# A two-layer graph network: how layer 0 of the kernel adds the rows of its edges per target node

## The chip, the cores and the metric

The kernel runs on one core of one Trainium2 chip. A core has five engines with an instruction stream each: PE (TensorE, matrix products), DVE (VectorE), ACT (ScalarE), POOL (GpSimd) and SP (SyncE, here only for issuing DMAs). They share the on-chip memory SBUF and the accumulator memory PSUM, and meet through semaphores. The metric is the device time of one execution in microseconds (us).

## The reference

12,500 nodes with 128 numbers each, 200,000 edges sorted by their target `dst`. Each layer normalises the nodes, sends a row along every edge, adds the rows per target, and applies two products.

```
h = relu(layernorm(x))
# layer 0
agg = segment_sum(h[src], dst, num_segments=12500)
x = x + (agg @ W_rel.T + b_rel + h @ W_root.T)
h = relu(layernorm(x))
# layer 1
edge_weights = silu(edge_attr @ We1 + be1) @ We2 + be2       # 50 -> 128 -> 128
agg = segment_sum(h[src] * edge_weights, dst, num_segments=12500)
x = x + (silu(agg @ Wn1 + bn1) @ Wn2 + bn2)
```

All of it is in fp32. A node has 16 incoming edges in the mean.

## The kernel before

**Tiles and stages.** The edges are cut into 391 blocks of 512, a block into 4 tiles of 128 edges, one edge per partition. Both layers run 23 iterations (`ITERS`) of 17 blocks (`U`). An iteration is cut into six groups (`G`) of three blocks (`GB`), the last group having two; a group is 12 tiles, the last 8, and 68 tiles make an iteration. For each group the lowest target is known (`sum_base`, `base_row`), and all of its targets are looked for in a window of 128 nodes from there. Were a group's targets spread wider, the whole layer would be run again with the windows moved by 128 (`passes`, from the table `plan` that DVE works out in the set-up).

**Gather (POOL).** `gather` issues one indirect DMA per tile, 68 per iteration (L320): 128 rows of 512 bytes into `rows`, which holds one iteration and is not doubled. Before the DMAs of group g POOL waits until the segment sums of the same group, one iteration earlier, have been signalled on `s_seg`. The indices come through SP (`load_idx`, L219) in two halves per iteration.

**Segment sum (DVE, PE).** For each group DVE's `one_hot` (L711) compares the targets in `dst_rel` with 0 to 127 and writes a 128x1536 one-hot matrix (1024 wide in the last group) into one of the two halves of `onehot`. PE's `segment_sum` (L370) multiplies each of the 12 tiles of rows by its one-hot tile and accumulates all of them in PSUM, in `seg_a` or `seg_b` by turns, and then signals `s_seg`. DVE's `add_window` (L719 to L723) waits for that and adds the 128x128 result to the right columns of `agg`. The order on DVE is written out by hand: `add_window` of group g-1, `one_hot` of group g+1, then a step of the node update.

**Set-up and the first iteration.** In the first 160 us the table of h = relu(layernorm(x)) is made for all nodes (`stats_of`, `shift_of`, `copy_h`: the h loop, 5 iterations of 5 node groups, L625 to L646), while POOL already gathers iteration 0 of layer 0. Since h is not ready then, iteration 0 gathers x and normalises the gathered rows itself (`edge_stats`, `edge_shift`, and ACT's relu; the edge phase). Iterations 1 to 22 gather from `h_rows`. Between its groups each of them also updates one group of 512 nodes (`node_update0`: ACT turns out `aggT`, PE makes 8 products L381 and L382 in group 1, DVE works on them in groups 3 to 5, L755 to L765). Three more updates follow the last iteration, then layer 1 begins.

**Layer 1.** The edge network (L410, L578, L416, L817, L825) makes each edge's message in `rows`, and `one_hot`, `segment_sum` and `add_window` add them as in layer 0.

## Time and profile before

| | us |
|---|---|
| median of 3 timed runs | 4831.68 (4816.43 to 4837.42) |
| the profiled execution's own time | 4849.66 |
| its span, first to last instruction | 4847.9 |
| POOL busy | 2970.8 (61%) |
| PE busy | 2418.4 (50%) |
| DVE busy | 1276.0 (26%) |
| ACT busy | 479.4 (10%) |

The profile is one execution. Its page gives each engine's busy time, the chain of work that ended last, and the costliest groups of instructions; the trace behind it gives each instruction with its start, its length, and how long the engine stood idle before it and for what. "remote" as a releaser means that the profile found no instruction on this core whose end fits the moment at which the waited semaphore rose; "issue" means that it shows nothing that the engine waited for. Times within the profile are counted from the span's start. The layers can be told apart by the lines: layer 0 ends on DVE at L704 and L705 near 2341 us.

### The profile page before, as it was taken

Reading aid. Unit: us, or ns where it says so; the run is one execution under the profiler, and the core shown is the slowest. Engines: PE = TensorE matmul, PEld = TensorE weight load, DVE = VectorE, ACT = ScalarE, POOL = GpSimd, SP = SyncE. Lnnn points to the kernel's source line nnn. Section 1 sums busy time; section 2 is a strip of 40 time slices with the busy share of each in tenths; the row PEclk is TensorE's granted clock in tenths of the full one; section 3 lists DMA queues with packets and bytes.
Section 4 is the critical chain, followed back from the end, with each engine's and each line's share of the span. In section 5 each row is a group of like instructions: output and inputs, shape, how many; then the busy total and the mean of one; then the engine's idle time right before and its main releaser. Section 6 shows DMA issues by size and latency. Waiting matters only on the chain.

```text
span 4847.9 us, 35780 instructions
## 1 busy us (share of the span) xinstructions
PE 2418.4 (50%) x10938; PEld 1841.8 (38%) x10938; DVE 1276.0 (26%) x2181; ACT 479.4 (10%) x842; POOL 2970.8 (61%) x3135
## 2 busy tenths in 40 slices
PE   1332323232323232322447677777666777767667
PEld 0322322232222222222334445555454555544545
DVE  2511111111111111111323333333333333333334
ACT  3400000000000000000101111111111111111111
POOL 5366666666666666666465656666656666656662
PEclk9755556555656565655667767777767777767777
DMA  5222222222221222222222222222222222222222
GB/s 135 61 53 52 55 53 56 54 53 53 56 54 51 56 55 54 51 56 55 62 59 61 65 62 64 65 69 64 65 61 64 65 67 66 64 61 64 64 63 59
DMA packets 230579, 296.77 MB, mean 61 GB/s; under 512 B 68580, under 2 KB 160278, under 8 KB 230433
## 3 DMA queue, kind: packets, MB, share of 16 engines
q0 software_dynamic: 100096, 205.20, 16.8%
q10 hardware_dynamic: 61378, 60.59, 4.6%
q1 hardware_dynamic: 69086, 30.79, 2.4%
q8 instruction: 6, 0.10, 0.0%
q14 instruction: 13, 0.10, 0.0%
HBM read 269.87 MB, written 26.48 MB: 61 GB/s over the span
## 4 chain that ended last, share of the span: by engine, by line
another core or an unknown queue 44%; PE 26%; issue 17%; DVE 10%; DVEq 2%; ACT 1%; POOL 0%; DMA 0%; ACTq 0%; SPq 0%; POOLq 0%
PE seg_a L370 7%; PE seg_b L370 5%; PE ew_a L416 4%; PE ew_b L416 3%; DVE onehot L711 3%; PE hid_b L410 3%; PE hid_a L410 2%; DVE ew_a L817 2%; DVE rows L825 2%; DVE ew_b L817 1%; DVEq L719 1%; PE node L430 0%; DVE e_stats L625 0%; PE node L381 0%
## 5 line engine op out<-in xcount | busy, mean ns | idle before, releaser
L320 POOL DMA_INDIRECT rows<-h_rows,idx x3060 | 2905.5, 950 | 1783.2 <-issue 952.2
L370 PE MATMUL seg_a<-onehot,rows 128*128 128x128 f32 x3312 | 662.9, 358 | 1136.9 <-DVE onehot L711 445.2
L370 PEld LDWEIGHTS seg_a<-onehot,rows 128*128 128x128 f32 x3312 | 601.9, 268 | 1221.4 <-issue 934.2
L370 PE MATMUL seg_b<-onehot,rows 128*128 128x128 f32 x2944 | 572.5, 340 | 809.3 <-issue 576.9
L370 PEld LDWEIGHTS seg_b<-onehot,rows 128*128 128x128 f32 x2944 | 504.8, 249 | 855.7 <-issue 659.9
L711 DVE TENSOR_TENSOR onehot<-iota_ps,dst_rel 128x1536 f32<-128x1536 f32 (+1 forms) x278 | 461.3, 1659 | 1.0 <-DVE dst_rel L699 0.6
L817 DVE TENSOR_TENSOR ew_a<-ew_a,be_all 128x512 f32<-128x512 f32 x207 | 144.6, 699 | 1044.7 <-remote 703.2
L416 PE MATMUL ew_b<-we_sb,hidden 128*128 128x128 f32 x1472 | 289.3, 357 | 224.6 <-ACT hidden L578 177.1
L416 PEld LDWEIGHTS ew_b<-we_sb,hidden 128*128 128x128 f32 x1472 | 245.2, 252 | 406.5 <-ACT hidden L578 210.3
L416 PEld LDWEIGHTS ew_a<-we_sb,hidden 128*128 128x128 f32 x1664 | 268.6, 245 | 246.3 <-issue 169.0
L416 PE MATMUL ew_a<-we_sb,hidden 128*128 128x128 f32 x1664 | 310.8, 345 | 81.4 <-ACT hidden L578 55.2
L723 DVE TENSOR_TENSOR agg<-seg_a,agg 128x128 f32 x138 | 40.3, 292 | 963.2 <-remote 883.0
L723 DVE TENSOR_TENSOR agg<-seg_b,agg 128x128 f32 x138 | 40.1, 290 | 866.1 <-remote 787.0
L817 DVE TENSOR_TENSOR ew_b<-ew_b,be_all 128x512 f32<-128x512 f32 x184 | 128.2, 697 | 508.1 <-remote 199.7
L578 ACT ACTIVATE hidden<-hid_a,be_col 128x512 f32<-128x512 f32 x208 | 142.9, 687 | 1106.9 <-remote 522.7
L578 ACT ACTIVATE hidden<-hid_b,be_col 128x512 f32<-128x512 f32 x185 | 126.9, 686 | 961.1 <-remote 486.7
L410 PE MATMUL hid_a<-ef_a,we_sb 50*128 50x512 f32 x278 | 196.9, 795 | 20.5 <-DMA ef_a<-ef_blocks 20.5
L410 PE MATMUL hid_b<-node_work,we_sb 50*128 50x512 f32 x230 | 173.1, 841 | 0.0
L825 DVE TENSOR_TENSOR rows<-ew_a,rows 128x512 f32<-128x512 f32 x207 | 143.2, 692 | 22.7 <-DMA rows<-h_rows,idx 13.2
L825 DVE TENSOR_TENSOR rows<-ew_b,rows 128x512 f32<-128x512 f32 x184 | 127.0, 690 | 7.9
L511 ACT ACTIVATE n_std<-n_mv,eps 128x4 f32<-128x4 f32 x25 | 7.4, 297 | 1041.4 <-issue 673.7
L523 ACT ACTIVATE hT<-agg 128x512 f32 x23 | 14.5, 629 | 851.3 <-DMA y_rows<-ys 845.7
(122 smaller groups left out, 1148.4 us busy)
## 6 DMA issues: line engine op xcount, KB each, us to landing
rows<-h_rows,idx POOLq DMA_INDIRECT x3060
ef_a<-ef_blocks ACTq DMA_DIRECT2D x70, 300.0 KB
node_work<-ef_blocks ACTq DMA_DIRECT2D x47, 300.0 KB
xs<-x SPq DMA_DIRECT2D x40, 256.0 KB
ys<-y_rows SPq DMA_DIRECT2D x26, 256.0 KB
out<-xs ACTq DMA_DIRECT2D x26, 256.0 KB
y_rows<-ys ACTq DMA_DIRECT2D x25, 256.0 KB
h_rows<-node_work ACTq DMA_DIRECT2D x23, 256.0 KB
```

Source lines behind the costliest of these rows:

```text
L320: pool.indirect_dma_start(out=rows[:, u, t, :], out_offset=None, in_=table, in_offset=bass.IndirectOffsetOnAxis(ap=idx[:, j:j + 1], axis=0 ...
L370: mm = pe.matmul(seg[g % 2][:, 0:P], rows[:, u, t, :], onehot[:, g % 2, k * TB + t, :], start=(k == 0 and t == 0), stop=(last and t == TB ...
L410: pe.matmul(hid_ps[u % 2][:, :], we1_sb[:, :], ef[g % 2][:, k, :], start=True, stop=True).then_inc(s_hid, 1)
L416: mm = pe.matmul(ew_ps[u % 2][:, t * D:(t + 1) * D], hidden[:, u % 2, t * P:(t + 1) * P], we2_sb[:, :], start=True, stop=True)
L511: nc.scalar.activation(n_std[:, r, :], n_mv[:, r, :, 1], ACT.Sqrt, bias=eps[:, :]).then_inc(s_nstd, 1)
L523: nc.scalar.activation(hT[r], h_table[:, bass.ds(g * BLOCK, BLOCK)], ACT.Copy)
L578: nc.scalar.activation(hidden[:, u % 2, :], hid_ps[u % 2][:, :], ACT.Silu, bias=be1_col[:, :]).then_inc(s_silu, 1)
L711: return v.tensor_tensor(onehot[:, g % 2, 0:tiles, :], iota_ps[:, 0:P].unsqueeze(1).to_broadcast([P, tiles, P]), dst_rel[:, bass.ds(it * U ...
L719: base = dve.value_load(base_row[0:1, bass.ds(it * G + g, 1)], min_val=0, max_val=BASE_MAX)
L723: v.tensor_tensor(window, seg[g % 2][:, 0:P], window, ALU.add).then_inc(s_acc[layer], 1)
L817: v.tensor_tensor(ew, ew, be2_all[:, :].unsqueeze(1).to_broadcast([P, TB, D]), ALU.add).then_inc(s_add, 1)
L825: v.tensor_tensor(rows[:, u, :, :], ew, rows[:, u, :, :], ALU.mult).then_inc(s_msg, 1)
```

## The change

In layer 0 the one-hot product over all tiles is replaced. The host arranges the edges so that a partition holds 12 neighbouring edges of the sorted list in each group (8 in the last group). Neighbours mostly have the same target, so a partition's 12 edges make a few runs of equal targets. `R = 3` runs are handled in one pass over the layer. In a new function `run_sums` DVE builds three masks of 12 columns in PSUM, `run_mask` (which edge belongs to which run), and a one-hot row for the target of each run, `run_hot` (128x384). Then, for each of the three runs, it multiplies the group's rows by the mask into a PSUM tensor of three banks (`wide`, 128x1536) and reduces that over the 12 edges into a 128x128 tile `run_sum`. The reduction reads PSUM with a stride of 128 numbers. PE then needs 3 products of 128x128 per group instead of 12 (8 in the last group). If a partition has more than three runs, the layer is run again with the next three (`passes0 = passes1 * ceil(runs / 3)`); the largest number of runs is worked out in the set-up.

What goes with it:

- POOL's gather in layer 0 waits on `s_sum`, which DVE's reductions raise, instead of PE's `s_seg`.
- DVE's `add_window` of group g-1 stands behind `run_sums` of group g. DVE now waits for the gathered rows; PE waits only for `s_sum`.
- The set-up counts the runs and finds their targets (`run_targets`, three rounds over the 1564 edge columns) ahead of the h loop, as now stand the clearing of `agg[0]`, the plan and the load of `dst_sb`.
- After a pass over layer 0 `next_turn` with one more `run_targets` takes the place of `next_pass`.
- `hid_a`, `hid_b` and `ew_a` of layer 1 become parts of `wide`; `iota_ps` shares a bank (`consts_ps`) with the masks. The rest of layer 1 is as before, with the edges in the new order.

```diff
+R = 3
+RUN_STEPS = 2 * R
+        run_now = consts_ps[:, P:P + R]
+        run_mask = consts_ps[:, 2 * P:2 * P + R * GB * TB].rearrange("p (r e) -> p r e", r=R)
+        wide = ctx.enter_context(nc.psum_tensor("wide", [P, GB * BLOCK], F32))
+        picked = wide[:, :].rearrange("p (e f) -> p e f", f=D)
...
@@ gather (POOL)
-                    hold(pool, s_seg[layer], i * G + (g + 1))
+                    if layer == 0:
+                        hold(pool, s_sum, runs_summed(i, g) - RUN_STEPS * G)
+                    else:
+                        hold(pool, s_seg[1], i * G + (g + 1))
...
@@ PE
+            def run_sums(i, g):
+                pe.wait_ge(s_sum, runs_summed(i, g))
+                for r in range(R):
+                    mm = pe.matmul(seg[g % 2][:, 0:P], run_sum[g % 2][:, r, :], run_hot[g % 2][:, r, :],
+                                   start=(r == 0), stop=(r == R - 1))
+                mm.then_inc(s_seg[0], 1)
...
@@ DVE, set-up
+            def run_targets(n):
+                for r in range(R):
+                    out = run_dst[:, :, r].rearrange("p (i g) -> p i g", g=G)
+                    v.scalar_tensor_tensor(scratch, run_of, run_now[:, r:r + 1], dst_flat,
+                                           ALU.is_equal, ALU.mult).then_inc(s_pass, 1)
+                    dve.wait_ge(s_pass, n + (2 * r + 1))
+                    v.tensor_reduce(out[:, :, 0:G - 1], per_run[:, :, 0:full].rearrange(
+                        "p i (g e) -> p i g e", g=G - 1), AX.X, ALU.max)
+                    v.tensor_reduce(out[:, :, G - 1], per_run[:, :, full:U * TB], AX.X, ALU.max).then_inc(s_pass, 1)
...
@@ DVE, layer 0
+            def run_sums(i, it, g):
+                dve.wait_ge(s_sum, done)
+                v.tensor_tensor(run_mask[:, :, 0:tiles],
+                                dst_rel[:, bass.ds(it * U + first, tiles // TB), :].rearrange("p k t -> p (k t)")
+                                .unsqueeze(1).to_broadcast([P, R, tiles]),
+                                run_now.unsqueeze(2).to_broadcast([P, R, tiles]),
+                                ALU.is_equal).then_inc(s_mask, 1)
+                v.tensor_tensor(run_hot[g % 2], iota_ps.unsqueeze(1).to_broadcast([P, R, P]),
+                                run_dst[:, bass.ds(it * G + g, 1), :].rearrange("p g r -> p (g r)").unsqueeze(2)
+                                .to_broadcast([P, R, P]), ALU.is_equal)
+                dve.wait_ge(s_mask, i * G + (g + 1))
+                for r in range(R):
+                    if r > 0:
+                        dve.wait_ge(s_sum, done + 2 * r)
+                    v.tensor_tensor(picked[:, 0:tiles, :],
+                                    rows[:, first:first + tiles // TB, :, :].rearrange("p k t f -> p (k t) f"),
+                                    run_mask[:, r, 0:tiles].unsqueeze(2).to_broadcast([P, tiles, P]),
+                                    ALU.mult).then_inc(s_sum, 1)
+                    dve.wait_ge(s_sum, done + (2 * r + 1))
+                    v.tensor_reduce(run_sum[g % 2][:, r, :], picked[:, 0:tiles, :].rearrange("p e f -> p f e"),
+                                         AX.X, ALU.add).then_inc(s_sum, 1)
...
                     for g in range(G):
+                        dve.wait_ge(s_rows[0][g], landed(i, g))
+                        run_sums(i, it, g)
                         if g > 0:
                             add_window(0, i, it, g - 1)
                         else:
                             add_window(0, i - 1, it - 1, G - 1)
-                        one_hot(it + (g + 1) // G, (g + 1) % G).then_inc(s_onehot, 1)
...
@@ host
+            order.append((first + g) * BLOCK + np.arange(P * tiles).reshape(P, tiles).T.ravel())
-    src_cols = src_pad.reshape(-1, P).T
+    src_cols = src_pad[order].reshape(-1, P).T
```

**DVE, one group of a layer-0 iteration.** Before, the row of DVE reads as follows from the one-hot of group 1 on; `TENSOR_LOAD base_row` fetches the window's column.

```order
233 L719 ISA
234 L719 TENSOR_LOAD base_row
235 L719 ISA x2
236 L721 ISA
237 L722 REGISTER_ALU [waits s_acc_done0]
238 L723 ISA [waits s_seg_done0]
239 L723 TENSOR_TENSOR agg<-seg_a,agg 128x128
240 L711 ISA
241 L711 TENSOR_TENSOR onehot<-iota_ps,dst_rel 128x1536
```

Of the changed kernel, the same place in the program, DVE on group 1 of an iteration:

```order
341 L824 ISA [waits s_rows0_1]
342 L825 ISA [waits s_sum]
343 L825 TENSOR_TENSOR consts_ps<-dst_rel,consts_ps 128x36
344 L830 ISA
345 L830 TENSOR_TENSOR onehot<-consts_ps,run_dst 128x384
346 L833 REGISTER_ALU
347 L837 TENSOR_TENSOR wide<-rows,consts_ps 128x1536 [waits s_mask]
348 L841 REGISTER_ALU
349 L842 TENSOR_REDUCE onehot<-wide 128x128 [waits s_sum]
...
360 L850 ISA [waits s_seg_done0,s_acc_done0]
361 L850 TENSOR_TENSOR agg<-seg_a,agg 128x128
```

The pair L837 and L842 stands there three times. Where DVE had two instructions per group with data to work on, it has nine, and the sum into `agg` now follows all of the group's own work.

**PE, groups 0 and 1 of a layer-0 iteration.** Before (`x11` is eleven more of the row above):

```order
85 L370 MATMUL seg_a<-onehot,rows 128x128 [waits s_rows0_0]
86 L370 MATMUL seg_a<-onehot,rows 128x128 x11
87 L378 ISA
88 L381 MATMUL node<-w_root_sb,hT 128x128 [waits s_nT]
89 L382 MATMUL node<-w_rel_sb,node_work 128x128
...
97 L370 MATMUL seg_b<-onehot,rows 128x128 [waits s_rows0_1,s_onehot]
98 L370 MATMUL seg_b<-onehot,rows 128x128 x11
```

and of the changed kernel:

```order
48 L399 MATMUL seg_a<-onehot 128x128 [waits s_sum]
49 L399 MATMUL seg_a<-onehot 128x128 x2
50 L415 ISA
51 L418 MATMUL node<-w_root_sb,hT 128x128 [waits s_nT]
52 L419 MATMUL node<-w_rel_sb,node_work 128x128
...
60 L399 MATMUL seg_b<-onehot 128x128 [waits s_sum]
61 L399 MATMUL seg_b<-onehot 128x128 x2
```

Nine of twelve products per group are gone; the node update's products stay where they were, ahead of the products of group 1.

## Rows read from the trace of the kernel before

**Rows 1.** Page, part 4: the chain that ended last, by engine.

```profile
another core or an unknown queue 44%; PE 26%; issue 17%; DVE 10%; DVEq 2%; ACT 1%; POOL 0%; DMA 0%; ACTq 0%; SPq 0%; POOLq 0%
```

**Rows 2.** Busy time by stretch (layer 0, layer 1): length, engines, clock, DMA share, GB/s.

```profile
500.00:2290.00 1790.00, 533.34 (x2752) 476.74 (x2752) 263.11 (x453) 57.31 (x130) 1181.26 (x1249) 0.58 0.21 54
2400.00:4800.00 2400.00, 1653.45 (x7061) 1177.52 (x7061) 795.23 (x1069) 300.85 (x425) 1463.45 (x1548) 0.71 0.25 64
```

**Rows 3.** Timeline of POOL, one layer-0 iteration: start, length, instruction, [idle before].

```profile
1026.44 0.95 POOL L320 DMA_INDIRECT rows<-h_rows,idx  x1 [6.83 <-remote]
...
1065.22 0.94 POOL L320 DMA_INDIRECT rows<-h_rows,idx  x1 [0.30 <-issue]
1072.55 0.94 POOL L320 DMA_INDIRECT rows<-h_rows,idx  x1 [6.39 <-remote]
...
1124.18 0.95 POOL L320 DMA_INDIRECT rows<-h_rows,idx  x1 [6.93 <-remote]
```

**Rows 4.** Timeline of DVE, the same iteration.

```profile
1071.92 0.29 DVE L723 TENSOR_TENSOR agg<-seg_b,agg 128x128 f32 x1 [34.80 <-remote]
...
1077.40 0.69 DVE L759 TENSOR_TENSOR xs<-node,xs 128x512 f32<-128x512 f32 x1
...
1123.54 0.29 DVE L723 TENSOR_TENSOR agg<-seg_a,agg 128x128 f32 x1 [39.14 <-remote]
```

**Rows 5.** Timeline of PE, the same iteration.

```profile
1047.82 0.37 PE L370 MATMUL seg_b<-onehot,rows 128*128 128x128 f32 x1 [1.73 <-issue]
...
1056.23 0.37 PE L370 MATMUL seg_a<-onehot,rows 128*128 128x128 f32 x1 [2.43 <-issue]
1059.04 0.37 PE L370 MATMUL seg_a<-onehot,rows 128*128 128x128 f32 x1 [2.44 <-issue]
...
1078.06 2.84 PE L370 MATMUL seg_a<-onehot,rows 128*128 128x128 f32 x24
```

**Rows 6.** Timeline of DVE in the set-up.

```profile
9.20 2.28 DVE L622 TENSOR_REDUCE hi_sb<-agg 128x4 int32<-128x2048 int32 x1
...
15.85 0.15 DVE L634 RECIPROCAL e_rstd<-e_std 128x4 f32<-128x4 f32 x1
20.47 0.16 DVE L636 SCALAR_TENSOR_TENSOR e_shift<-e_mv,e_rstd 128x4 f32<-128x4 f32 x1 [4.47 <-remote]
...
34.94 0.86 DVE L625 BATCH_NORM_STATS2 e_stats<-node_work 128x6 f32<-128x128 f32 x4
41.64 0.38 DVE L629 BATCH_NORM_AGGREGATE e_mv<-e_stats 128x2 f32<-128x6 f32 x4 [5.84 <-remote]
```

**Rows 7.** Timeline of DVE 19 us into an unbroken stretch of gathers in layer 0.

```profile
292.44 0.88 DVE L736 BATCH_NORM_STATS2 n_stats<-xs 128x6 f32<-128x128 f32 x4
293.42 0.38 DVE L740 BATCH_NORM_AGGREGATE n_mv<-n_stats 128x2 f32<-128x6 f32 x4
```

**Rows 8.** Timeline of POOL: iterations 0, 1 and 2 begin, and layer 0's last gather.

```profile
3.61 1.10 POOL L320 DMA_INDIRECT rows<-x,idx  x1 [2.17 <-issue]
...
174.34 0.95 POOL L320 DMA_INDIRECT rows<-h_rows,idx  x1 [85.83 <-PE seg_a L370]
...
273.27 0.94 POOL L320 DMA_INDIRECT rows<-h_rows,idx  x1 [6.41 <-remote]
...
2320.03 0.94 POOL L320 DMA_INDIRECT rows<-h_rows,idx  x1 [0.30 <-issue]
```

**Rows 9.** Timeline of DVE: memory cleared, targets, first and last one-hot of the edge phase.

```profile
143.87 10.72 DVE L656 MEMSET agg<- 128x12800 f32 x1 [2.62 <-issue]
...
159.11 1.60 DVE L695 TENSOR_TENSOR dst_rel<-dst_sb,sum_base 128x1380 f32<-128x1380 int32 x1 [1.63 <-issue]
...
161.60 1.76 DVE L711 TENSOR_TENSOR onehot<-iota_ps,dst_rel 128x1536 f32<-128x1536 f32 x1 [0.63 <-DVE dst_rel L699]
...
232.80 1.75 DVE L711 TENSOR_TENSOR onehot<-iota_ps,dst_rel 128x1536 f32<-128x1536 f32 x1
```

**Rows 10.** Instructions of L704, one at the end of each pass over a layer.

```profile
L704 DVE TENSOR_SCALAR dst_rel<-dst_rel x2: 981/981/981, 2340.4 to 4836.7; 128x1576 f32<-128x1576 f32 x2
```

More of the change, by code:

```diff
@@ L372, in segment_sum @@
                 if last:
-                    mm.then_inc(s_seg[layer], 1)
+                    mm.then_inc(s_seg[1], 1)
             def node_update0(n, r):
@@ L437, in _ @@
             edge_weights(0, 0)
-            with pe.Fori(0, passes) as p:
+            with pe.Fori(0, passes1) as p:
                 with pe.Fori(0, ITERS) as it:
@@ L582, in _ @@
             load_ef(0, 1)
-            with act.Fori(0, passes) as p:
+            with act.Fori(0, passes1) as p:
                 with act.Fori(0, ITERS) as it:
@@ L639, in _ @@
+            run_targets(0)
             with dve.Fori(0, GROUPS // H_SETS) as k:
@@ L853, in edge_blocks @@
                         steps[u]()
-            with dve.Fori(0, passes) as p:
+            with dve.Fori(0, passes1) as p:
                 one_hot(0, 0)
@@ L884 @@
     ef_pad[:N_EDGES] = edge_attr_50
-    src_cols = src_pad.reshape(-1, P).T
-    ef_cols = ef_pad.reshape(N_BLOCKS, BLOCK, D_EDGE).transpose(0, 2, 1)
+    order = []
+    for first in range(0, N_BLOCKS, U):
+        for g in range(0, U, GB):
+            tiles = min(GB, U - g) * TB
+            order.append((first + g) * BLOCK + np.arange(P * tiles).reshape(P, tiles).T.ravel())
+    order = np.concatenate(order)
+    src_cols = src_pad[order].reshape(-1, P).T
+    ef_cols = ef_pad[order].reshape(N_BLOCKS, BLOCK, D_EDGE).transpose(0, 2, 1)
     arrays = {
```

249 lines of the change are left out of this document (160 added, 89 removed).

## The prediction

> **What bounds the kernel now.** First the chain of waits: its largest share, 44%, is "another core or an unknown queue" [rows 1]. There is no other core, so the profile doesn't know what releases these waits. The table by stretch shows next that no engine is full in layer 0: POOL is busy for 1181 of 1790 us, PE for 533, DVE for 263 [rows 2]. So I followed one iteration on each engine.
>
> POOL issues its 68 gathers in two unbroken stretches, 32 from 1026.44 to 1066.2 and 36 from 1072.55 to 1117.3, one per 1.25 us (0.95 busy, 0.30 issue), and waits for 6.39 and 6.93 us between them [rows 3]. An iteration is 1124.18 − 1026.44 = 97.7 us: 85.0 of gathers and 13 of waits. The waits are for `s_seg`, released as "remote".
>
> DVE shows the same signal: it stood 34.8 us for `seg_b` until 1071.92 and 39.1 us for `seg_a` until 1123.54 [rows 4]. Yet PE had recorded the last product of that `seg_b` at 1047.82, and those of the `seg_a` by 1080.9 [rows 5]. (A product of one tile leaves two MATMUL rows, so x24 is a group.) The signals came 24 and 42 us after the products, each some 6 us after POOL had fallen silent. Within the stretches PE's rows stand singly, every 2.8 us, "issue" before them, where the 24 together took 2.84 us [rows 5]. This is the pattern that decides: **some way into an unbroken stretch of gathers an engine with much in hand gets its completions slowly, until about 6 us after the stretch ends.** DVE shows it in the set-up, where gathers run from 3.61 on [rows 8]: what it finished at 16.0 it could use only at 20.47, and the four `bn_stats` of 34.94 only at 41.64 [rows 6]. With the one instruction before them that is 5 in 6.7 us, 1.3 us each. But an engine with little in hand is spared: 19 us into a stretch of layer 0 DVE ran four `bn_stats` and read them at once [rows 7]; there it has 25 instructions with data per iteration (two per group and 13 of the node update). I don't know the mechanism; it behaves like an allowance that is spent faster than it comes in. On PE 2.8 us per single row is 1.4 us for each weight load and each product.
>
> Layer 0 ends with POOL's last gather, at 2321.0 [rows 8], and a tail of 20.4 us up to the end of L704 at 2341.4 [rows 10]. Layer 1 follows, and is the same code after the change.
>
> **The change, part by part.**
>
> *POOL.* The 85.0 us of gathers per iteration stay. Only the waits can go.
>
> *DVE, a full group.* Removed: a one-hot of 1.75 us [rows 9]. Added: the mask, 0.2; `run_hot`, 384 wide, 0.5 (512 wide 0.69 [rows 4]); three multiplications of 1536 numbers, one input in SBUF and one in PSUM as in the one-hot, 1.75 each; three reductions. A contiguous one of 2048 took 2.28 [rows 6], so 1536 give 1.75. Each of these six waits for the one before, some 0.07. That is 0.7 + 6 × 1.82 = 11.6, and with 0.5 for the addition to `agg` and its register load 12.1 us; a group of 8 tiles comes to 8.9. With 4.0 for the node update an iteration costs DVE 5 × 12.1 + 8.9 + 4.0 = **73.4 us**. It lies beside 85 us of gathers, since a buffer is wanted again only an iteration later: hidden while it stays under 85. What no row shows is the reduction's read of PSUM with a stride of 128 numbers. From below I see no gain against the contiguous row; from above I take twice its time, 3.5 us. I take 1.75: one number per partition in 1.1 ns is what all of DVE's long rows have in common, from SBUF and PSUM, int32 and fp32 [rows 6, 9].
>
> The Trainium skill speaks against this read (SBUF — State Buffer, the note on cachelines after the table of ports): PSUM has 8-byte cachelines, and "any non-contiguous PSUM access pattern significantly slows down matmuls". That is said of matmuls, and no row here has such a read. If it held for DVE, the time would be that of rival 2 instead of the forecast's.
>
> *Completions.* DVE goes from 25 instructions with data per iteration to 9 × 6 + 13 = 67. Were it slowed all the time, at 1.3 us each that would be 87 us, hardly above 85. PE has 68 tiles and 8 products of the node update per iteration now: 76 × 2 products and as many weight loads, 304. After the change it has 18 + 8, so 104. At 1.4 us each an unbroken iteration of 85 us lets through 61 of them. Now the other 243 go through in and around the two waits, some 120 each; then 104 − 61 = 43 need 0.4 of a wait of 6.7 us, 2.4 us per iteration, and at most a whole one. DVE's slowed rate gives 2 by itself. I take 4, so **an iteration is 89 us**, bounds 87 and 91.
>
> *PE.* Its recorded work shrinks to a third and was not on the path; nothing is taken for it. DVE's addition of group g−1 now waits behind the runs of g, which gives PE's signal 12 us more before anyone wants it. Behind that wait stand DVE's next masks, and for the sums made from them POOL waits only five groups later, cover of some 70 us.
>
> *Set-up.* New or moved ahead of the h loop on DVE: the clearing, 10.7 [rows 9]; seven steps over 1564 columns at 1.0 to 1.8 (1.60 for 1380 [rows 9]), 10; `run_targets`, three rounds of a step of 1.8 and a reduction of 1.9, 11.5 with its end; the plan and small steps, 5. That is 37 us, or 50 to 60 with slowed completions (45 instructions × 1.3). It lies within the first stretch of gathers, 3.61 to 88.6, where the h loop is slow anyway; what is pushed behind 88.6 runs fast. Behind the h loop 17 us are gone (clearing, plan, targets). The edge phase could thus begin between 145 (all new work hidden) and 185 (none), against 161.6; I take 150. The edge phase itself, 161.6 to 232.8 [rows 9], grows by 12.1 − 1.75 − 0.5 = 9.9 for five groups and 7 for the last, 56 us, of which slowed completions that it already shows cover about 10: 71 + 46, to 267. It frees the buffers for POOL's iteration 1 group by group, and the last gathers end near 267 + 3 + 10 + 3 = 283, where iteration 2 began at 273.3 [rows 8]. **Cost: 10 us.**
>
> *Tail.* After the last gather: 2.5 for the rows to land, 8.9 for the last group, 1.5 for PE and the addition, 14 for `next_turn` (8 small steps and `run_targets`): 27 us instead of 20.4.
>
> *Layer 1* has the same gathers and tiles, in another order of edges: nothing.
>
> **Sum.** 283 + 21 × 89 + 27 = 2179, against 2341.4: −162 us. From the profiled execution's 4849.7 that gives 4687; the median of the runs is 18 lower, 4831.7, so I give **4669**.
>
> **The rivals.**
> 1. *Completions never hold POOL up*: the new counts stay within the allowance, as DVE's 25 do now. 85 us per iteration: 283 + 1785 + 27 = 2095, −246, **4585**. For it: rows 7. Against: PE's 104 against 61.
> 2. *The strided reduction is slow, and DVE becomes the bound (slower than before).* At twice the contiguous time it costs 1.75 more, for 17 full ones per iteration 29.8 us: DVE needs 103.2, and the edge phase grows as well. 283 + 30 + 21 × 103.2 + 27 = 2507, +165, **4997**. With c more per reduction the end is 310 + 17c + 21 × (73.4 + 17c); it passes 2341.4 at c = 1.3, a reduction of 3.1 us.
> 3. *The waits stay.* PE's products of the node update stand ahead of the sums of group 1; 32 instructions at 1.4 us there could bring DVE, and then POOL, to two waits per iteration as now. The 2048 us from iteration 2 to the last gather stay: 283 + 2048 + 27 = 2358, +16, **4848**.
> 4. *Layer 0 runs twice*, with more than three runs on a partition, +2000 us. In the reference's own sorted targets 6,396 pairs of partition and group have one run, 11,118 two, 150 three, none more; and each layer makes one pass [rows 10]. Left out.
>
> **How the numbers follow.** Forecast, 87 to 91 us per iteration, 4627 to 4711: 0.48. Rival 1: 0.20. In between the forecast and rival 3, 92 to 96 us: 0.06. Rival 3: 0.09. Rival 2: 0.17, with 0.01 of it within the bound. 0.5%, 24 us, is about what a measurement of this kernel can tell from no change. Faster: 0.48 + 0.20 + 0.06 = 0.74. Same: 0.10. Slower: 0.16. The range leaves out most of rival 2 and a few hundredths below rival 1: 4575 to 4870.
>
> **What would show it.** Right: POOL's two waits of over 6 us per layer-0 iteration become one or fewer; L837 and L842 take about 1.75 us each; DVE is busy some 73 us per iteration and its additions no longer stand for 35; iteration 2 begins at 275 to 290. Wrong: L842 at 3 us or more and POOL waiting for DVE (rival 2); "remote" ahead of DVE's additions and POOL's waits as now (rival 3); or waits of over a microsecond between L837 and L842, by which completions that are late add to DVE's chain of six waits per group instead of lying beside it, a cost that the sum leaves out.

## Result and profile after: slower by 4.8%

The changed kernel takes 5067.05 us (median of 4 runs, 5057.75 to 5073.23) against 4830.77 for the kernel before. The ratio is 1.0482, 95% interval 1.0453 to 1.0510. The prediction was 4669, range 4575 to 4870: wrong in sign.

The profiled execution has a span of 5055.9 us, 208 more than before. Busy times and the chain of waits, from the page of the changed kernel:

```profile
PE 2059.6 (41%) x8640; PEld 1505.2 (30%) x8640; DVE 2554.6 (51%) x3188; ACT 481.2 (10%) x842; POOL 2970.5 (59%) x3135
DVE 29%; another core or an unknown queue 27%; PE 19%; issue 15%; DVEq 7%; ACT 1%; DMA 0%; ACTq 0%; SPq 0%
```

The unknown releaser fell from 44% [rows 1] to 27%, and DVE stands in the chain for 29%. POOL's gathers are as many and as long as before.

The timeline of POOL shows the new pattern (start, length, instruction, and in brackets the idle time before it and its releaser). Before there were two waits of 6.4 and 6.9 us in an iteration [rows 3]. Now there is one long wait, and short ones of 1 to 2 us:

```profile
1040.23 0.94 POOL L349 DMA_INDIRECT rows<-h_rows,idx  x1 [1.38 <-DVE onehot L842]
1074.87 0.94 POOL L349 DMA_INDIRECT rows<-h_rows,idx  x1 [19.97 <-DVE onehot L842]
1147.21 0.94 POOL L349 DMA_INDIRECT rows<-h_rows,idx  x1 [1.82 <-DVE onehot L842]
1181.17 0.94 POOL L349 DMA_INDIRECT rows<-h_rows,idx  x1 [19.29 <-DVE onehot L842]
```

The distance of the long waits, 1181.17 − 1074.87 = 106.3 us, is an iteration. Over 20 iterations the mean is 106.26 us, 21.3 more than its 85.0 us of gathers, against 97.52, 12.5 more, before. What releases POOL is L842, the last reduction of `run_sums`. DVE's timeline shows why that comes so late:

```profile
1062.48 0.29 DVE L850 TENSOR_TENSOR agg<-seg_b,agg 128x128 f32 x1 [23.03 <-remote]
1062.77 0.20 DVE L825 TENSOR_TENSOR consts_ps<-dst_rel,consts_ps 128x36 f32<-128x36 f32 x1
1062.91 0.56 DVE L830 TENSOR_TENSOR onehot<-consts_ps,run_dst 128x384 f32<-128x384 f32 x1
...
1072.35 1.76 DVE L842 TENSOR_REDUCE onehot<-wide 128x128 f32<-128x1536 f32 x1
```

And PE's timeline of the products of that `seg_b`, and of the next ones:

```profile
1020.57 1.65 PE L399 MATMUL seg_b<-onehot 128*128 128x128 f32 x6 [11.59 <-issue]
...
1039.51 1.65 PE L399 MATMUL seg_a<-onehot 128*128 128x128 f32 x6 [17.30 <-DVE onehot L842]
...
1074.16 1.65 PE L399 MATMUL seg_b<-onehot 128*128 128x128 f32 x6 [33.00 <-DVE onehot L842]
```

PE recorded the three products (six rows) by 1022.2. DVE saw the signal only at 1062.48, 40 us later, and 7.6 us after POOL had fallen silent at 1074.87 − 19.97 = 1054.90. Up to there this is the old pattern [rows 4, 5]. But what PE's signal once released was POOL itself. Now it releases `add_window` on DVE, and behind that stands `run_sums` of the next group, 11.3 us from 1062.77 to 1074.11, for which POOL waits. The wait adds up as 7.6 to the late signal, 0.3 for the addition, 11.3 for the run sums and 0.8 until POOL starts: 20.0.

### The profile page after: what moved, and what is told of

It is laid out like the page before. It is cut to its first block, busy times and chain, and to the rows that moved or that the text cites. A ratio compares the mean times of both kernels' runs of the same rounds, so it can differ in the third digit from the quotient of the medians.

```text
span 5055.9 us, 32959 instructions
## 1 busy us (share of the span) xinstructions
PE 2059.6 (41%) x8640; PEld 1505.2 (30%) x8640; DVE 2554.6 (51%) x3188; ACT 481.2 (10%) x842; POOL 2970.5 (59%) x3135
## 4 chain that ended last, share of the span: by engine, by line
DVE 29%; another core or an unknown queue 27%; PE 19%; issue 15%; DVEq 7%; ACT 1%; DMA 0%; ACTq 0%; SPq 0%
DVE wide L837 12%; DVE onehot L842 7%; PE wide L441 6%; PE wide L447 4%; PE ew_b L447 3%; PE seg_a L407 3%; DVEq L846 3%; PE seg_b L407 3%; DVE wide L943 2%; DVE rows L951 1%; DVE ew_b L943 1%; DVE onehot L812 1%; DVEq L841 1%; DVE onehot L830 1%
## 5 line engine op out<-in xcount | busy, mean ns | idle before, releaser
L837 DVE TENSOR_TENSOR wide<-rows,consts_ps 128x1536 f32<-128x1536 f32 (+1 forms) x414 | 691.7, 1671 | 46.4 <-issue 36.8
L842 DVE TENSOR_REDUCE onehot<-wide 128x128 f32<-128x1536 f32 (+1 forms) x414 | 690.4, 1668 | 14.4
L609 ACT ACTIVATE hidden<-wide,be_col 128x512 f32<-128x512 f32 x393 | 266.4, 686 | 2056.6 <-remote 1028.8
L407 PE MATMUL seg_a<-onehot,rows 128*128 128x128 f32 x1656 | 316.0, 353 | 262.7 <-DVE rows L951 230.6
L407 PEld LDWEIGHTS seg_a<-onehot,rows 128*128 128x128 f32 x1656 | 289.2, 263 | 278.2 <-DVE rows L951 246.1
L407 PE MATMUL seg_b<-onehot,rows 128*128 128x128 f32 x1472 | 278.6, 351 | 218.1 <-DVE rows L951 147.1
L447 PEld LDWEIGHTS wide<-we_sb,hidden 128*128 128x128 f32 x1664 | 267.8, 244 | 238.0 <-issue 166.0
L447 PE MATMUL wide<-we_sb,hidden 128*128 128x128 f32 x1664 | 310.3, 345 | 69.4 <-ACT hidden L609 47.9
L441 PE MATMUL wide<-ef_a,we_sb 50*128 50x512 f32 x418 | 289.6, 779 | 27.5 <-DMA ef_a<-ef_blocks 27.5
L441 PE MATMUL wide<-node_work,we_sb 50*128 50x512 f32 x368 | 264.6, 806 | 3.5 <-issue 3.5
```

Source lines behind the costliest of these rows:

```text
L407: mm = pe.matmul(seg[g % 2][:, 0:P], rows[:, u, t, :], onehot[:, g % 2, k * TB + t, :], start=(k == 0 and t == 0), stop=(last and t == TB ...
L441: pe.matmul(hid_ps[u % 2][:, :], we1_sb[:, :], ef[g % 2][:, k, :], start=True, stop=True).then_inc(s_hid, 1)
L447: mm = pe.matmul(ew_ps[u % 2][:, t * D:(t + 1) * D], hidden[:, u % 2, t * P:(t + 1) * P], we2_sb[:, :], start=True, stop=True)
L609: nc.scalar.activation(hidden[:, u % 2, :], hid_ps[u % 2][:, :], ACT.Silu, bias=be1_col[:, :]).then_inc(s_silu, 1)
L837: v.tensor_tensor(picked[:, 0:tiles, :], rows[:, first:first + tiles // TB, :, :].rearrange("p k t f -> p (k t) f"), run_mask[:, r, 0:tile ...
L842: v.tensor_reduce(run_sum[g % 2][:, r, :], picked[:, 0:tiles, :].rearrange("p e f -> p f e"), AX.X, ALU.add).then_inc(s_sum, 1)
```

## Experiments

**Theory.** (1) In long unbroken stretches of gathers PE's and DVE's completions are held back, as before, and the waited signal arrives some 7 us after POOL stops. (2) The change has put DVE's run sums, 11.5 us, between that signal and POOL, so a wait costs 20 instead of 6.5 us. "Held" below is a name for the pattern in the traces: recorded work whose signal comes late, or instructions that stand singly with "issue" before them. **Rivals:** DVE's new work is simply too much for an iteration; or it is DVE's own completions that are late and not PE's; or the number of PE's instructions decides whether a wait comes at all, as the prediction had it.

### The probe: what is held

A kernel of its own (nothing of the reference is computed), in nine sections: 200 one-column writes on DVE, alone and beside 48 gathers; 60 products on PE beside gathers; DVE and ACT together; writes that begin in the middle of a stretch; writes beside direct DMAs; gathers of 64-byte rows; chained writes; empty instructions.

> Not the network: nine sections, each after some 20 us without work, to see when engines are slowed. (1) 200 tiny DVE writes alone. (2) the same beside 48 gathers of 128 x 512 bytes. (3) 60 products on PE beside 48 gathers. (4) 100 tiny writes on DVE and 100 on ACT beside 48 gathers. (5) 200 DVE writes that begin at gather 25. (6) 200 beside 48 direct DMAs of 64 KB. (7) 200 beside 48 gathers of 64-byte rows. (8) 80 writes each waiting for the one before, beside gathers. (9) ten times 15 empty instructions and a write, beside gathers. Allowance theory: in (2) some 50 instructions pass at full rate (0.06 us), the others at 1.3 us; (5) the same, from its own start; (1) and (6) at full rate throughout. Age theory (it begins some 12 us into a stretch of gathers): (5) is slow from its first instruction. If the allowance is shared among the engines, (4) gets slow on both after some 25 each.

Measured: 656.51 us. DVE in windows of 4 us (window, its length, DVE's busy time and rows, PE's granted clock, DMA share, GB/s), first alone, then beside gathers that start at 40.41:

```profile
16.00:20.00 4.00, 2.32 (x97) 1.00 0.03 4
...
40.00:44.00 4.00, 2.01 (x86) 1.00 0.12 33
44.00:48.00 4.00, 0.65 (x38) 1.00 0.20 51
52.00:56.00 4.00, 0.32 (x14) 1.00 0.22 55
60.00:64.00 4.00, 0.27 (x7) 1.00 0.19 49
64.00:68.00 4.00, 0.19 (x5) 1.00 0.19 49
```

The same writes run at 97 in 4 us alone, and beside gathers at 86, 38, 14, 7 and 5. The 200 writes took 6 us alone and 31 us here. Late in the stretch the rows stand 0.65 or 1.34 us apart, "issue" before them:

```profile
60.40 0.09 DVE L92 MEMSET dv<- 128x1 f32 x3 [1.34 <-issue]
61.83 0.06 DVE L92 MEMSET dv<- 128x1 f32 x1 [1.34 <-issue]
```

Writes that begin 15 us into a stretch (284.88 to 299.76) had 24 within 0.7 us, so they are not slow from their first instruction, but then hardly any: 25 in the first 4 us and 10 in the next. Beside direct DMAs all 200 were done in 5.5 us at up to 135 GB/s, twice the traffic (beside gathers 136 in the same time). Beside gathers of 64-byte rows (9 GB/s) they slowed as much as beside those of 512 bytes:

```profile
300.00:304.00 4.00, 0.79 (x25) 0.50 0.19 49
304.00:308.00 4.00, 0.29 (x10) 0.50 0.27 67
...
374.00:378.00 4.00, 2.42 (x86) 0.50 0.48 135
412.00:416.00 4.00, 2.36 (x104) 0.50 0.05 6
432.00:436.00 4.00, 0.20 (x5) 0.50 0.10 9
```

So it goes with indirect gathers, not with the bytes they move. PE had 64 matmul rows in 10 us and then 17 in 28, a tenth of the rate, while its granted clock was 1.00 and then 0.51. ACT had 9 rows in 8 us beside DVE and 37 in the next 8, when DVE was done. That looks as if the engines shared what is let through; it is one observation. 81 chained writes and 150 empty instructions passed unslowed, but all within the first 10 us of their stretches, so they tell nothing of its later part. What the mechanism is, no row tells. "Allowance" in the prediction remains a description.

### One run instead of three: is the 11.5 us in the wait?

```diff
-RUN_STEPS = 2 * R
+RUN_STEPS = 2
...
-                for r in range(R):
+                for r in range(1):
```

On DVE only; the sums of the second and third runs are left out.

> The changed kernel with one run instead of three on DVE in each group of layer 0 (the multiply and the reduction of the second and third run are left out, PE still makes its three products, so the sums are incomplete). DVE has 7.2 us less per group and four instructions with data less. Edge phase: about 40 us less either way. Theory A: the wait of POOL shrinks by just the 7.2 us that DVE needs less behind PE's late signal, 20 to 13, iteration 99 us: about 4870 us. Theory B (DVE is the bound): DVE has 41 us less per iteration, the wait disappears, 85 to 87 us: about 4610 us.

Measured, in one run: 4845.42 us (before, same chip: 4839.41), iteration 98.20, 13.2 us over the gathers instead of 21.3. Two pairs of multiplication and reduction are 2 × 3.6 = 7.2 us; the iteration is 8.1 us shorter, near the expectation and far from the 85 to 87 of a DVE that is simply too slow. But there is no longer one wait in each iteration. From 750 us on they come in every second one, and there are two kinds. From the timelines of DVE and POOL:

```profile
997.56 0.29 DVE L850 TENSOR_TENSOR agg<-seg_b,agg 128x128 f32 x1 [27.03 <-remote]
1000.24 1.76 DVE L842 TENSOR_REDUCE onehot<-wide 128x128 f32<-128x1536 f32 x1
```

```profile
943.84 0.94 POOL L349 DMA_INDIRECT rows<-h_rows,idx  x1 [12.48 <-issue]
1002.77 0.94 POOL L349 DMA_INDIRECT rows<-h_rows,idx  x1 [14.31 <-DVE onehot L842]
```

The second is the wait of the theory. POOL was silent from 988.46; it is 9.1 us to the late signal, 0.3 for the addition, 4.1 for the one run (1002.00 − 997.85) and 0.8 until POOL starts: 14.3. This shows point (2): DVE's work behind the signal stands in POOL's wait at full length, 4.1 us here and 11.3 in the changed kernel. It also shows that the signal doesn't always come 7 us after POOL's silence. The first wait, 12.5 us before group 0 of an iteration, has nothing to do with the run sums: DVE's reduction had ended 6.6 us before POOL went on. SP issues the load of new indices, for which POOL waits there as well, at 942.6, and at the first such wait (362.10) the profile names that load. So it seems that SP's signal can be late too. That the total came out near 7.2 us less is in part luck.

### add_window one group later

Three buffers instead of two for `run_hot`, `run_sum` and PE's result, and `add_window` of group g−2 behind `run_sums` of g, so that PE's signal has an additional group of time. The product of the node update moves to group 2.

```diff
-        run_hot = [run_slots[:, R * k:R * k + R, :] for k in range(2)]
+        run_hot = [run_slots[:, R * k:R * k + R, :] for k in range(3)]
+        seg0 = [seg[0][:, 0:P], seg[1][:, 0:P], ew_ps[1][:, 0:P]]
...
-                        if g > 0:
-                            add_window(0, i, it, g - 1)
+                        if g > 1:
+                            add_window(0, i, it, g - 2)
```

> The changed kernel, with the addition of a group's window two groups behind its run sums instead of one (three buffers for run_sum, run_hot and the PSUM result; the node update's product one group later). Theory A (coupling): the changed kernel's one wait of 20 us per layer-0 iteration is 7.4 us until PE's held signal comes after POOL fell silent, plus 11.6 us of run sums that stand on DVE behind the wait for that signal. With 12 us more cover DVE waits less or not at all, and an iteration falls from 106.3 us to 85 to 93: 4630 to 4790 us in all. Theory B (DVE is the bound by its many instructions, each of them slowed during gathers): nothing is won, 106 us and 5050 to 5070.

Measured: 4921.90 (4890.99 to 4924.72) against 4839.41, ratio 1.0148 (1.0113 to 1.0183): most of the loss is gone, but it doesn't beat the kernel before, and it is neither the 85 to 93 us of the one theory nor the 106 of the other. The iteration is 98.79 us with two waits in the mean, of 3.4 to 15.7 us, 13.8 in all. DVE's groups of instructions, 500 to 1900 us (count | busy, mean ns | idle before, by releaser), of the changed kernel:

```profile
L825 DVE TENSOR_TENSOR consts_ps<-dst_rel,consts_ps 128x36 f32<-128x36 f32 (+1 forms) x78 | 15.4, 197 | 71.6 <-issue 71.6
...
L850 DVE TENSOR_TENSOR agg<-seg_b,agg 128x128 f32 x39 | 11.2, 288 | 315.0 <-remote 298.0 <-issue 17.0
```

and of this experiment, where the same two are L826 and L851:

```profile
L826 DVE TENSOR_TENSOR consts_ps<-dst_rel,consts_ps 128x36 f32<-128x36 f32 (+1 forms) x86 | 17.1, 198 | 147.3 <-issue 145.4 <-PE seg_b L400 1.2 <-DVE agg L851 0.7
...
L851 DVE TENSOR_TENSOR agg<-seg_b,agg 128x128 f32 x29 | 8.3, 287 | 62.1 <-issue 62.1
L851 DVE TENSOR_TENSOR agg<-seg_a,agg 128x128 f32 x29 | 8.3, 286 | 71.1 <-issue 71.1
```

The 298 us of "remote" are gone: DVE no longer stands for PE. In their place "issue" has grown, 145 us before the mask alone: DVE's own instructions, the register loads and arithmetic between the groups among them, are now held. With that DVE has become the bound: of these 1400 us it is busy for 996 and stands for "issue" for another 382. So the rival of too much work on DVE is right here, but only with the hold: its busy time alone would fit into the 85 us of gathers. Layer 0 also ends later after its last gather: the next layer's first gather comes 104.8 us behind it (2337.6 to 2442.4), against 47.8 in the kernel before (2320.0 to 2367.8) and 94.1 in the changed one, since DVE is several groups behind.

### Loops written out

In the changed kernel DVE and PE work out columns and semaphore values in registers, in a loop. Written out, these are constants.

```diff
-            with dve.Fori(0, passes0) as p:
+            for p in (0,):
...
-                with dve.Fori(1, ITERS) as it:
+                for it in range(1, ITERS):
```

The same on PE. First the changed kernel so, then the kernel before, then the changed one with the later `add_window` as well.

> The changed kernel with the loops over passes and iterations of layer 0 written out on DVE and PE (one pass assumed, as the data has), so that the waits are for constants and the register instructions that worked the numbers out are gone: some 150 rows of DVE per layer-0 iteration become some 95, PE's 104 weight loads and products stay. Theory A (only PE's held signal and DVE's run sums behind it count): the wait of 20 us stays, 104 to 106 us per iteration, 5020 to 5070 us. Theory B (DVE too loses time for each row of its own, register instructions included, as the gaps of 0.8 to 3.3 us before L825, L837 and L850 suggest): 90 to 98 us, 4730 to 4900 us.

> The kernel before with the same loops written out on DVE and PE (one pass). Its PE has 304 weight loads and products and only some 15 register rows per iteration, so nothing changes: 97 to 98 us, 4820 to 4850 us. If register rows are what is slow, it falls below 95 us, under 4780.

> Both edits together: the loops written out and the addition of the window two groups behind. In e1 the added cover took 7.5 us per iteration, and DVE then was slowed by its own rows. If A and B are the two causes and nothing else, DVE's wait and its gaps are both gone and an iteration is 85 to 90 us: 4620 to 4740 us, faster than both kernels. If a third thing holds POOL up, it stays near the 98.8 us of e1: 4920.

Measured, with 4835.94 for the kernel before: the changed kernel 5016.21 (one run; iteration 104.58, one long wait of 18.6 in the mean), the kernel before 4839.90 (one run; 97.33, no change), the last one 4986.98 (4980.04 to 4993.86), ratio 1.0303 (1.0275 to 1.0332), iteration 102.82 where 85 to 90 was expected. DVE's groups of the first, 500 to 1900 us:

```profile
L825 DVE TENSOR_TENSOR consts_ps<-dst_rel,consts_ps 128x36 f32<-128x36 f32 (+1 forms) x79 | 14.9, 189 | 0.5 <-issue 0.5
...
L850 DVE TENSOR_TENSOR agg<-seg_b,agg 128x128 f32 x40 | 11.4, 285 | 501.4 <-remote 501.4
```

"Issue" before L825 fell from 71.6 to 0.5, and all that DVE waited stands for PE's signal, 501.4. So DVE's own slowness came with its register instructions. But taking it away gave POOL 1.7 us of 106.3 only: DVE reaches the wait for PE earlier and stands there until the same moment after POOL's silence. The third shows both limits at once, and is slower than the later `add_window` alone (4922). Its long wait has moved to the node update, where DVE wants PE's product of group 2:

```profile
1048.07 0.70 DVE L883 TENSOR_TENSOR node<-node,b_rel_all 128x512 f32<-128x512 f32 x1 [17.09 <-remote]
```

### Fewer products on PE

In the kernel before, 3 of the 12 products of a group (the others are left out); in the changed kernel 1 of 3, and in the node update only the second of the two products, that with w_rel.

```diff
-                for t in range(TB):
+                for t in range(first, TB):
```

> The kernel before, with 3 of the 12 tile products per group in layer 0 (2 blocks of the last group: 3 of 8), the others left out, so that PE has 104 rows per iteration as in the changed kernel and the signals still go straight to POOL. Theory of the prediction (completions are held once an allowance is used up, so it is PE's count that brings two waits per iteration): the waits shrink from 13 us to 7 or less per iteration, 85 to 92 us: 4560 to 4710 us. Rival (any signal of PE is held in a long stretch, whatever its count): 97.7 us, 4830.

> The changed kernel with one of the three products per group and, in the node update of layer 0, only the product with w_rel (the others left out): 40 instead of 104 rows of PE per iteration. Theory A as refined (PE's signal is late because PE's own rows wait to be completed): the signal comes in time, DVE no longer stands 23 us, POOL's waits fall from 20 to 10 us or less, 90 to 96 us per iteration, 4730 to 4850 us. If the signal is held by the gathers as such, whatever PE has to do: 106 us, 5060.

Measured, in one run each: the kernel before with a quarter of its products 4797.40 (4839.41 whole), iteration 95.34, 10.3 us over the gathers instead of 12.5. By the prediction's reckoning with counts, this should have come near 89; by the rival, it should have stayed at 97.7. POOL's groups, 500 to 1900 us, of the whole kernel before and then of this one:

```profile
L320 POOL DMA_INDIRECT rows<-h_rows,idx x977 | 924.0, 946 | 474.8 <-issue 289.3 <-remote 185.4
```

```profile
L320 POOL DMA_INDIRECT rows<-h_rows,idx x999 | 947.3, 948 | 453.6 <-issue 299.3 <-remote 154.3
```

A quarter of the products leaves 154.3 of 185.4 us of waiting. The number of waits fell as reckoned, to one per iteration in the mean, but their sum much less. They mostly come in pairs in every second iteration, one of 3 to 4 us and then, after only 12 gathers, one of 18 to 19:

```profile
1025.10 0.94 POOL L320 DMA_INDIRECT rows<-h_rows,idx  x1 [3.55 <-remote]
1058.11 0.94 POOL L320 DMA_INDIRECT rows<-h_rows,idx  x1 [18.33 <-remote]
```

Here the signal comes 17.7 us after POOL's silence (DVE's addition at 1057.48, silence from 1039.78), not 6. How long after it the signal comes is thus no constant either.

The changed kernel with few products took 4900.76, iteration 98.92 (90 to 96 expected), 13.9 us over the gathers. Here DVE's waits for PE are gone without any change to the order. So the number of PE's instructions does matter: with 104 rows per iteration its signal was late, with 40 it is not. DVE's own instructions are now what is late, and DVE is full, 1006 us busy and 384 of "issue" out of 1400:

```profile
L824 DVE TENSOR_TENSOR consts_ps<-dst_rel,consts_ps 128x36 f32<-128x36 f32 (+1 forms) x86 | 17.1, 199 | 156.7 <-issue 156.0 <-DVE agg L849 0.7
...
L849 DVE TENSOR_TENSOR agg<-seg_a,agg 128x128 f32 x43 | 12.3, 287 | 96.8 <-issue 95.6 <-PE seg_b L399 1.2
```

So two things hold POOL up, and each covers the other: PE's late signal (seen alone with the loops written out) and DVE's held instructions (seen alone with few products, or with the later addition). Removing either leaves iterations of 99 to 105 us. That they are all is not shown: removing both by the later addition and the written-out loops gave 102.8 us, with a third wait, for PE's product of the node update.

### Both causes at once, and the chips that hold nothing

Two kernels were to remove both, and that third wait. One is the written-out kernel with the later `add_window` and the few products of the last experiment (part of the sums is left out). The other keeps the whole computation and moves the node update's product to group 3 and its later steps into the next iteration:

```diff
-                return {2: product}
+                return {3: product}
...
+                    steps = {5: steps[3]}
+                    if it > 1:
+                        late = node_update0(n - 1, 0, n)
+                        steps[0], steps[1] = late[4], late[5]
```

> e5 (loops written out, addition two groups behind) with the PE work of e6 (one of three products per group, and only the product with w_rel in the node update of layer 0; the others left out). e5 took 102.8 us per iteration with DVE waiting 5 and 17 us for signals of PE, e6 took 98.9 with DVE losing 4 to 6 us at a time before its own rows. If PE's held signals and DVE's own held rows are the two causes, and either alone is enough to make POOL wait, then with both cut an iteration is 85 to 89 us: 4560 to 4660 us. If there is a third cause, it stays above 95 us: over 4780.

> e5 with the node update spread wider: PE's product at group 3, DVE's step on it at group 5, the shift and the last addition in groups 0 and 1 of the next iteration. It takes DVE's 17 us wait for PE's node product away, which stood at group 3. Expected by the two causes: 102.8 falls by the 8 to 17 us of that wait, to 87 to 96 us: 4600 to 4830 us. If the wait only moves on to the window additions: 100 to 103 us, 4920 to 4990.

With them ran a second probe, writes on DVE beside gathers with pauses of different lengths:

> Not the network: seven sections of 60 gathers with 250 tiny DVE writes beside them from the start. (0) gathers without a pause, (1) one small iota of POOL after each gather, (2) four, (3) 24 iotas after each 12 gathers, (4) 12 after each 6, (5) gathers of 32 rows instead of 128, (6) 48 iotas after each 24 gathers. By p1, without pauses some 130 writes pass in the first 5 us, and then the rate falls to one per 1.3 us. If what slows DVE is worked off in POOL's pauses, the late rate rises with them in (2) to (4) and (6), and most where a pause is longest. If it is the number of descriptors, (5) is slowed a quarter as much.

Measured: 4049.47 and 4058.48, but the kernel before took 4004.72 on this chip, not 4836. The probe took 719.70, and in each of its sections the 250 writes beside gathers were done within 7.5 us; from the first (DVE's, then POOL's busy time and rows):

```profile
18.00:23.00 5.00, 4.43 (x157) 3.67 (x4) 1.00 0.15 39
```

This chip holds no completions. So these runs tell nothing about the two causes. The two variants were run on two more chips, with the changed kernel and the probe beside them on the one and the kernel before on the other. Both chips were of the same kind.

> The changed kernel once more, unedited. On a chip that holds completions (the kernel before at 4830 us): 106 us per layer-0 iteration, 5060. On a chip that doesn't (the kernel before at 4005): if the sizes worked out for DVE's part are right and held completions are the whole of the rest, POOL never waits in layer 0 in either kernel, 85 us per iteration in both, and what is left is the longer edge phase (some 30 us) and next_turn (14 us): 4040 to 4065 us, 1 to 1.5% slower. If something else in the change makes POOL wait: over 4150.

> e8 again: loops written out, addition two groups behind, one of three products per group and half of the node update's products on PE (the others left out). On a chip that holds completions: if PE's held signals and DVE's held rows are the two causes, 85 to 90 us per iteration, 4560 to 4680 us; a third cause: over 4780. On one that doesn't: 4049 as before.

> e9 again: loops written out, addition two groups behind, the node update spread over the next iteration. On a chip that holds completions: 87 to 96 us per iteration and 4600 to 4830 us if DVE's 17 us wait for the node product was the rest; 100 to 103 us and 4920 to 4990 if it moves to the window additions. On one that doesn't: 4058 as before.

> The seven sections of 60 gathers with 250 tiny DVE writes again. On a chip that doesn't hold completions all writes pass in under 10 us in each section, as before. On one that does: some 130 writes in the first 5 us, then fewer and fewer; if POOL's pauses work the backlog off, sections (3), (4) and (6) end sooner than (0), and section (5), with a quarter of the descriptors, is slowed less.

> The kernel before, unedited, for its trace on this chip. Where no completions are held (its total 4000 us): 85 us per iteration in layer 0 as in layer 1, POOL without a wait; layer 0 ends about 50 us before that of the changed kernel. Where they are held: 97.5 us and 105, 4830 us, with two waits of 6.4 us per layer-0 iteration.

> e8 a third time. Where completions are held: if PE's held signals and DVE's held rows are the two causes of POOL's wait, 85 to 90 us per layer-0 iteration, 4560 to 4680 us; with a third cause over 95 us and 4780. Where they are not: 4050.

> e9 a third time. Where completions are held: 87 to 96 us per layer-0 iteration, 4600 to 4830 us, if DVE's 17 us wait for the node product was the rest of e5; 100 to 103 us, 4920 to 4990, if that wait moves to the window additions. Where they are not: 4052.

Measured: the changed kernel 4047.06 (4044.61 to 4048.27) against 3997.78, ratio 1.0121 (1.0104 to 1.0138), as expected; the two variants 4053.39 and 4051.94, the latter 1.0132 (1.0116 to 1.0149); the probe 715.50; the third time the kernel before 3998.22 (and 4000.38 beside it), the variants 4056.35 and 4054.16. That the hold is the chip's is seen best in one stretch of the kernel before, whose work there is the same, 4 to 88 us (busy and rows of PE, weight loads, DVE, ACT and POOL, then clock, DMA share, GB/s), first in the trace of the prediction, then on the third of the others:

```profile
4.00:88.00 84.00, 6.69 (x24) 4.29 (x24) 17.18 (x82) 14.32 (x34) 63.56 (x68) 1.00 0.51 134
```

```profile
4.00:88.00 84.00, 27.88 (x100) 17.87 (x100) 62.27 (x274) 55.82 (x139) 63.59 (x68) 1.00 0.84 237
```

POOL does the same 68 gathers. Beside them DVE gets through 82 rows on the one, 274 on the other. In layer 0 PE's signal comes straight after its products there (DVE's timeline): "PE" is named as releaser, not "remote", and POOL waits no more:

```profile
723.42 0.29 DVE L723 TENSOR_TENSOR agg<-seg_a,agg 128x128 f32 x1 [12.91 <-PE seg_a L370]
```

```profile
L320 POOL DMA_INDIRECT rows<-h_rows,idx x1116 | 1060.5, 950 | 340.1 <-issue 340.1
```

(The second is POOL's group of 500 to 1900 us.) The changed kernel's register instructions are in place there too, and "issue" before L825 in the same stretch is 3.0 us instead of 71.6:

```profile
L825 DVE TENSOR_TENSOR consts_ps<-dst_rel,consts_ps 128x36 f32<-128x36 f32 x99 | 19.6, 198 | 251.9 <-DMA rows<-h_rows,idx 248.9 <-issue 3.0
```

An iteration is 85.3 us before, 84.9 after the change: nothing but gathers, and nothing to gain. What stays is the change's cost at the two ends: iteration 2 begins at 231.7 instead of 191.3, because the edge phase now has run sums on which POOL waits, and from the last gather to the end of the layer it is 29 instead of 9.7 us. Of the 40 at the start 32 are left at the last gather (2012.8 against 1980.7); with 19 at the end that is 51, where the times differ by 49.

## The prediction, step by step

**What bounds the kernel** (completions held during long stretches) was right, and the probe shows it without the kernel. The conclusion from it was wrong.

**DVE's cost**: right. The strided reduction takes 1.76 us like the multiplication, the chain of six steps has no gap in it when nothing is held, and a group's run sums take 11.3 us for 11.6. (One reading was loose: 1.1 ns a number is not common to all of DVE's long rows. The clearing of 12,800 numbers took 10.72 us [rows 9], 0.84 ns each, and L704's 1576 took 0.98 us [rows 10]. Nothing hung on it.) From DVE's timeline:

```profile
1009.78 1.76 DVE L837 TENSOR_TENSOR wide<-rows,consts_ps 128x1536 f32<-128x1536 f32 x1 [0.88 <-issue]
1011.58 1.76 DVE L842 TENSOR_REDUCE onehot<-wide 128x128 f32<-128x1536 f32 x1
```

Rival 2 is thereby out. POOL did come to wait for DVE, as it said, but by another mechanism. The Trainium skill's note on cachelines (SBUF — State Buffer, after the table of ports) speaks of matmuls, and this trace shows nothing like it on DVE: 1536 numbers read at a stride of 512 bytes in PSUM took 1.76 us, no more than the multiplication of as many.

**Set-up and edge phase**: the edge phase began at 149 us (150 predicted) and ended at 250 (267). Iteration 2 began at 265.6 (283), 8 us before its time in the kernel before. On the chips that hold nothing the same work moved it back by 40 us, so here waits that were there anyway cover nearly all of it, where the sum let them cover 10:

```profile
148.99 0.87 DVE L657 BATCH_NORM_STATS2 e_stats<-rows 128x6 f32<-128x128 f32 x4 [1.42 <-ACT agg L520]
...
250.20 0.28 DVE L850 TENSOR_TENSOR agg<-seg_a,agg 128x128 f32 x1
```

**The step that failed** is *Completions*: "43 need 0.4 of a wait of 6.7 us", and with it 89 us for an iteration. It measured 106.26, +363 us over 21 iterations: the waits cost 21.3 us per iteration, where the sum took 4. Two things were wrong in it. First, the length of a wait was taken over from the kernel before, though the same text had moved the releaser: it said of PE's late signal that behind it "stand DVE's next masks, and for the sums made from them POOL waits only five groups later". That cover was counted from the moment at which DVE arrives at its wait. But the signal comes only after POOL has stopped, and POOL stops only when the cover is used up. The missing term is DVE's 11.3 us of run sums, read off the timeline, and 4.1 us where only one run is summed. Second, PE's count: at the 104 rows that the change leaves, the signal is still late, and a single late signal is enough for the wait. With a quarter of its products, as many rows, the kernel before still had 10.3 us of waits per iteration, where the same reckoning took 4. Only at 40 rows did DVE's waits for PE vanish.

The last sentence on what would show it wrong, late completions that add to DVE's chain, came nearest: "issue" of 0.8 to 3.3 us stands before the additions, the masks and the first multiplications, though not between L837 and L842. In the changed kernel that is the smaller part, about 2 us of the iteration by the written-out loops.

**Tail**: 27 predicted, 73.6 measured (from the last gather's end at 2496.8 to that of L718 at 2570.4). DVE comes to the last gather five groups behind, and the estimate assumed one. **Layer 1**: nothing, as said (104.3 us per iteration in the mean, 104.7 before). The sum: −17 at the start, +363 and +46 make 2571 out of 2179. Against before, layer 0 is 229 us longer, and 21 us come back from its end to that of the kernel.

**Rival 3** had the right reason and gave 4848: it kept the two waits but also their length. **Rival 1**'s iteration of 85 us is what the other chips show, but there it holds for the kernel before too. The forecast had no case in which a chip holds nothing; on such a chip it would have been wrong as well, by a loss of 1.2%.

**Open:** what holds the completions, why on some chips only, and whether the recording of instructions for the profile has a part in it, which no run here tells; what sets how long after POOL's silence a signal comes (6 to 18 us); and whether POOL is free of waits when both causes are removed on a chip that holds them. A kernel that is faster than the one before was not found on either kind.

## What to carry to other kernels

When a change makes another engine the one that frees a buffer, price the wait anew: it is the time until the late signal plus all that now stands between that signal and the release. Work that is "hidden beside the gathers" is not hidden if it is queued behind a wait which ends only when the gathers stop. And where a wait shows no releaser in the trace, look on another chip before tuning for it: here 17% of the time was gone there. Last, when an experiment's total comes out as reckoned, look at the single waits before taking it as proof: with one run on DVE the total was right, and half of the waits were others.

## Of the hardware

- Whether completions are held beside indirect gathers depends on the chip: the kernel before took 4831 to 4839 us in three sets of runs and 3998 to 4005 in three others, with gathers of the same 1.25 us.
- Instructions that read and write registers go with the hold on DVE: written out, 71.6 us of "issue" before the masks became 0.5; on a chip that holds nothing they were 3.0 with the registers in place.
- The late signal comes only after POOL has fallen silent, but not at a fixed distance: 6 us in the kernel before, 7.6 in the changed one, 9.1 with one run on DVE, 17.7 with a quarter of the products.
- A gather of 128 rows of 64 bytes takes POOL as long as one of 512 bytes: 0.95 us and 0.30 between two.
- DVE's multiplication and its reduction both take 1.76 us for 1536 numbers per partition, about 1.15 ns each, though the reduction reads PSUM at a stride of 512 bytes.
